# First image: layer-0 input halves seven chunks ahead, row ends ahead of the statistics, Newton steps of two images on VectorE

## What is computed

```python
x = x + _L0_conv_ref(_gn(x), w_fft_real, w_fft_imag, rot_w, rot_b, bn_gamma, bn_beta)
x = x + _L1_conv_ref(_gn(x), weight)
```

## Time and profile before

| | |
|---|---|
| median of 3 runs | 1798.08 us (1795.96 to 1798.11) |
| profiled execution, its own time | 1799.18 us |
| its span in the trace | 1797.4 us |
| mean granted PE clock (share of 2.4 GHz) | 0.977 |
| PE busy | 1655.8 us (92%) |
| DVE busy | 1388.3 us (77%) |
| ACT busy | 1172.3 us (65%) |
| POOL busy | 128.1 us (7%) |
| chain that ended last | PE 72%, DVE 14%, issue 5%, DMA 5% |
| L500 hi0, ACT | 264 of 1137 ns |
| L684 lo0, DVE | 264 of 1259 ns |
| L848 lo1, DVE | 264 of 1262 ns |
| L886 bn_stats, DVE | 454 of 687 ns |

### The profile page before, as it was taken

How to read it: one execution, slowest core, us unless ns; L and a number is a source line. 1 busy time by engine, 2 the same in 40 slices (tenths; PEclk the granted TensorE clock), 3 DMA queues, 4 the chain that set the end, 5 groups by cost and what they waited for, 6 DMA issues and landing times.

```text
span 1797.4 us, 65352 instructions
## 1 busy us (share of the span) xinstructions
PE 1655.8 (92%) x29275; PEld 1246.7 (69%) x29275; DVE 1388.3 (77%) x2175; ACT 1172.3 (65%) x1044; POOL 128.1 (7%) x361
## 2 busy tenths in 40 slices
PE   5887888487779999999999999999999999999899
PEld 5787888333356667887688668866786678666655
DVE  6989999779878787877887888787888788787500
ACT  6888888468556666666666666666666666666444
POOL 0000000120110010002000200020002001100100
PEclk9999999789899999999999999999999999999999
DMA  9999999355446665656666666566656665665245
GB/s 386 421 422 422 422 422 422 146 156 152 126 138 212 206 193 192 218 190 197 207 207 203 188 211 211 198 191 214 202 193 198 206 207 192 202 206 193 96 193 201
DMA packets 101782, 411.56 MB, mean 229 GB/s; under 512 B 16883, under 2 KB 19496, under 8 KB 85160
## 3 DMA queue, kind: packets, MB, share of 16 engines
q1 hardware_dynamic: 100744, 407.81, 64.6%
q0 software_dynamic: 800, 0.15, 0.1%
HBM read 271.82 MB, written 136.07 MB: 227 GB/s over the span
## 4 chain that ended last, share of the span: by engine, by line
PE 72%; DVE 14%; issue 5%; DMA 5%; POOL 1%; ACT 1%; SPq 1%; DVEq 0%; POOLq 0%; ACTq 0%
PE ps L406 36%; PE ps L399 34%; DVE x L635 7%; DMA x<-x_pix 5%; DVE nat L684 2%; DVE x L848 2%; DVE stats L886 1%; ACT x L475 1%; PE ps L350 0%; PE ps L351 0%; SPq L248 0%; PE ps L358 0%; POOL sm L606 0%; DVE ps L854 0%; PE ps L354 0%
## 5 line engine op out<-in xcount | busy, mean ns | idle before, releaser
L399 PE MATMUL ps<-nat,wc 64*64 64x512 f16 (+1 forms) x12480 | 1269.1, 379 | 45.7 <-DVE nat L684 16.5
L406 PE MATMUL ps<-x,wc 64*64 64x512 f16 (+2 forms) x12585 | 1256.4, 375 | 15.3 <-POOL x L615 14.8
L399 PEld LDWEIGHTS ps<-nat,wc 64*64 64x64 f16 x12480 | 721.8, 107 | 252.6 <-issue 38.2
L406 PEld LDWEIGHTS ps<-x,wc 64*64 64x64 f16 x12585 | 732.2, 107 | 193.4 <-POOL x L615 18.5
L500 ACT ACTIVATE nat<-xin,gnp 128x1024 f16<-128x1024 f32 (+1 forms) x264 | 299.9, 1137 | 318.6 <-PE ps L399 306.1
L848 DVE SCALAR_TENSOR_TENSOR x<-ps,gnp,x 128x1024 f16<-128x1024 f32 (+1 forms) x264 | 333.1, 1262 | 28.7 <-ACT x L515 21.5
L530 ACT ACTIVATE outb<-ps,bias 128x1024 f32<-128x1024 f32 (+1 forms) x264 | 289.7, 1097 | 88.5 <-PE ps L406 72.8
L684 DVE SCALAR_TENSOR_TENSOR nat<-xin,gnp,nat 128x1024 f16<-128x1024 f32 (+1 forms) x264 | 332.3, 1259 | 2.0 <-ACT nat L500 1.9
L519 ACT ACTIVATE x<-ps,gnp 128x1024 f16<-128x1024 f32 (+1 forms) x231 | 252.8, 1095 | 107.1 <-DVE stats L886 106.6
L350 PE MATMUL ps<-x 128*128 128x129 f16 x2048 | 258.0, 226 | 59.3 <-DVE x L635 59.2
L635 DVE SCALAR_TENSOR_TENSOR x<-x 128x2048 bf16<-128x2048 f32 x128 | 284.1, 2285 | 17.3 <-ACT x L475 15.6
(11 more groups left out here) (125 smaller groups left out, 273.6 us busy)
## 6 DMA issues: line engine op xcount, KB each, us to landing
x<-x_pix SPq DMA_DIRECT2D x128, 1024.0 KB, 13.5
xin<-x_tiles SPq DMA_DIRECT2D x256, 512.0 KB, 3.8
out<-outb SPq DMA_DIRECT2D x256, 512.0 KB, 4.1
xin<-x_tiles SPq DMA_DIRECT2D x8, 192.5 KB, 2.4
out<-outb SPq DMA_DIRECT2D x8, 192.5 KB, 3.7
w<-taps_scratch SPq DMA_DIRECT2D x64, 8.0 KB, 1.8
w<-taps_scratch SPq DMA_DIRECT2D x28, 16.0 KB, 2.7
taps_scratch<-x POOLq DMA_DIRECT2D x21, 3.0 KB, 3.4
```

The lines of the kernel that those rows point to most:

```text
L399: return nc.tensor.matmul(ps[64 * kind:64 * kind + 64, bank, 0:w], lhs, nat[rows, xhl, a:a + w], start=first, stop=last)
L406: ins = nc.tensor.matmul(ps[64 * kind:64 * kind + 64, bank, done:done + part], lhs, x1[rows, xhl, z:z + part], start=first and done == 0, ...
```

## The change

- `NB = 3`: image 0 has seven input slots, NFIRST0 = 7, instead of four: four in `nat`, three in slots 33 to 35 of the `x1` ring, which image 0's results don't use (`nat_at`). The start of slot 4's chunk is copied behind slot 3, and that of slot 0's chunk behind slot 6 (`nat_end`), each as two instructions, one for each half; in the later images too the copy is two instructions.
- ACT does hi0 of chunks 0 to 6 ahead of its loop, DVE lo0 of 0 to 3, `weights0(0)`, then pad and lo0 of 4 to 6, then pad(7). In the loop `ahead(g)` gives g+7 up to g = 25, nothing for g = 26 to 28, and g+4 from g = 29 on.
- The buffers of the pixel phase move, so that they keep clear of what is written early.
- POOL does `row_ends(b)` before it waits for `seeded`.
- For images 0 and 7 (`ALONE`) the Newton turns and `alpha` are done by DVE (`newton1`), right behind `spread`, with `weights1` right behind that; for the others POOL does them as before.

```diff
@@ -33,7 +33,8 @@
 PASSES = [(whl, xhl, dj) for whl, xhl in ((0, 0), (1, 0), (0, 1)) for dj in range(2)]
 NX = 4
 NO = 3
-AHEAD = 4
+NB = 3
+NFIRST0 = NX + NB
 LAG = NCH + 2
 RING = NCH + 4
 RCOLS = RING * CH
@@ -41,6 +42,7 @@
 SLOTS = 4
 TRAIL = 2
 GN_EPS, BN_EPS = 1e-5, 1e-5
+ALONE = (0, B - 1)
 YS = 16.0
 WS = 64.0
 X1S = YS * WS
@@ -106,6 +108,13 @@
     if _g >= LAG:
         JOB1[_g - LAG] = len(JOBS)
         JOBS.append((1, _g - LAG))
+
+
+def ahead(g):
+
+    if g + NFIRST0 < NCH:
+        return g + NFIRST0
+    return g + NX if g + NX >= NCH and g + NX < ALL else None
 
 
 def l1_chunk(h):
@@ -158,12 +167,14 @@
             return big[0:parts, a:a + width]
 
         apix = early(ASLOTS * ACHUNK).rearrange("p (s n) -> p s n", s=ASLOTS)
+        assert at_[0] + 256 <= NCH * CH // 2
+        TAPS_AT = at_[0]
+        tapsb = early(256, 9 * B)
+        at_[0] = RCOLS // 2
         gmask = early(B * P).rearrange("p (b q) -> p b q", b=B)
         colsum, gcol, gtmp = early(B), early(1), early(P)
         gram = early(B * C, C).rearrange("p (b c) -> p b c", b=B)
         zpad = early(400)
-        tapsb = early(256, 9 * B)
-        TAPS_AT = at_[0]
         early(at_[0] % 2)
         alo = early(AROUND * ACHUNK // 2).bitcast(BF16).rearrange("p (s k c) -> p s k c", s=AROUND, k=ABLK)
         ahi = early(AROUND * ABLK * (P + 2) // 2).bitcast(F16).rearrange("p (s k c) -> p s k c", s=AROUND, k=ABLK)
@@ -172,8 +183,8 @@
         wfs = early(256, 2 * K3)
         zt, zu = early(9 * B, 2 * K3), early(9 * B, 2 * K3)
         zc = early(384)
-        assert at_[0] <= RCOLS
-        TAPS_SLOT = min((TAPS_AT - 256) // (CH // 2), RING - 1)
+        assert at_[0] <= RCOLS // 2 + NCH * CH // 2
+        TAPS_SLOT = TAPS_AT // (CH // 2)
 
         def c(name, parts=P):
             if name in COL:
@@ -270,6 +281,19 @@
 
             return (g % RING) * CH
 
+        def nat_at(g):
+
+            spot = g % NFIRST0 if g < NCH else g % NX
+            return (nat, spot * CH) if spot < NX else (x1, (NCH + spot - NX) * CH)
+
+        def nat_end(g):
+
+            if g < NCH and g % NFIRST0 == 0:
+                return (x1, (NCH + NB) * CH)
+            if (g % NFIRST0 == NX) if g < NCH else (g % NX == 0):
+                return (nat, NX * CH)
+            return None
+
         @block.sync
         def _(sp):
             for dst, src in ((cst[:, :], consts), (first, firsts), (rw[:, :], rotw), (smallp[:, :], small),
@@ -395,8 +419,9 @@
                 bank = CB * (job % SLOTS) + q
                 lhs = (wc0 if layer == 0 else wc1)[rows, (i // NCH) % 2, whl, kind, dj, :]
                 if layer == 0:
-                    a = (i % NX) * CH + off
-                    return nc.tensor.matmul(ps[64 * kind:64 * kind + 64, bank, 0:w], lhs, nat[rows, xhl, a:a + w],
+                    planes, a = nat_at(i)
+                    a += off
+                    return nc.tensor.matmul(ps[64 * kind:64 * kind + 64, bank, 0:w], lhs, planes[rows, xhl, a:a + w],
                                             start=first, stop=last)
                 a = x1_slot((i // NCH) * NCH + n) + off
                 done = 0
@@ -495,9 +520,11 @@
                 b, n = divmod(g, NCH)
                 w = CH if n < NFULL else EDGE
                 act.wait_ge(pad_done, g + 1)
-                if g >= NX:
-                    act.wait_ge(pe_done, JOB0[g - NX] + 1)
-                nc.scalar.activation(nat[:, 0, (g % NX) * CH:(g % NX) * CH + w], xin[:, g % NX, 0:w], ACT.Identity,
+                last = g - (NFIRST0 if g < NCH else NX)
+                if last >= 0:
+                    act.wait_ge(pe_done, JOB0[last] + 1)
+                planes, a = nat_at(g)
+                nc.scalar.activation(planes[:, 0, a:a + w], xin[:, g % NX, 0:w], ACT.Identity,
                                      scale=gnp[:, 1, b:b + 1]).then_inc(hi0_ready, 1)
 
             def hi1(g):
@@ -530,14 +557,14 @@
                 nc.scalar.activation(outb[:, h % NO, 0:writes(n)], psum_of(JOB1[h], writes(n)), ACT.Identity,
                                      bias=bias[:, b % 2:b % 2 + 1], scale=1.0 / (HS * X1S)).then_inc(o_done, 1)
 
-            for g in range(NX):
+            for g in range(NFIRST0):
                 hi0(g)
             for g in range(ALL + LAG):
                 early = g < ALL and g >= NCH and by_act(*divmod(g, NCH))
                 if early:
                     hi1(g)
-                if g + NX < ALL:
-                    hi0(g + NX)
+                if ahead(g) is not None:
+                    hi0(ahead(g))
                 if g < ALL and not early:
                     hi1(g)
                 if g >= LAG:
@@ -600,13 +627,14 @@
                     upto = TROWS if n == NFULL else (n + 1) * CH // PITCH
                     column_ends(b, rows, upto)
                     rows = upto
+                row_ends(b)
                 pool.wait_ge(seeded, b + 1)
-                for turn in range(3):
-                    link(G.tensor_scalar(stat["h"], stat["y"], stat["half"], stat["y"], ALU.mult, ALU.mult))
-                    link(G.tensor_scalar(stat["y"], stat["h"], 1.5, stat["y"], ALU.add, ALU.mult))
-                G.tensor_scalar(stat["alpha"], stat["y"], X1S, gnp[:, 4, b:b + 1], ALU.mult, ALU.mult
-                                ).then_inc(alpha_ready, 1)
-                row_ends(b)
+                if b not in ALONE:
+                    for turn in range(3):
+                        link(G.tensor_scalar(stat["h"], stat["y"], stat["half"], stat["y"], ALU.mult, ALU.mult))
+                        link(G.tensor_scalar(stat["y"], stat["h"], 1.5, stat["y"], ALU.add, ALU.mult))
+                    G.tensor_scalar(stat["alpha"], stat["y"], X1S, gnp[:, 4, b:b + 1], ALU.mult, ALU.mult
+                                    ).then_inc(alpha_ready, 1)
                 link(G.tensor_scalar(stat["cc"], stat["d"], stat["M"], gnp[:, 5, b:b + 1], ALU.add, ALU.mult))
                 link(G.tensor_copy(chl[:, 0:1], stat["cc"]))
                 link(G.tensor_tensor(chl[:, 1:2], stat["cc"], chl[:, 0:1], ALU.subtract))
@@ -679,14 +707,17 @@
 
                 b, n = divmod(g, NCH)
                 w = CH if n < NFULL else EDGE
-                a = (g % NX) * CH
+                planes, a = nat_at(g)
+                end = nat_end(g)
                 ve.wait_ge(hi0_ready, g + 1)
-                ins = V.scalar_tensor_tensor(nat[:, 1, a:a + w], xin[:, g % NX, 0:w], gnp[:, 1, b:b + 1],
-                                             nat[:, 0, a:a + w], ALU.mult, ALU.subtract)
-                if g % NX == 0:
-
+                ins = V.scalar_tensor_tensor(planes[:, 1, a:a + w], xin[:, g % NX, 0:w], gnp[:, 1, b:b + 1],
+                                             planes[:, 0, a:a + w], ALU.mult, ALU.subtract)
+                if end is not None:
+
+                    copy, z = end
                     after(post(ins))
-                    ins = V.tensor_copy(nat[:, :, NX * CH:NX * CH + NXT], nat[:, :, 0:NXT])
+                    for part in range(2):
+                        ins = V.tensor_copy(copy[:, part, z:z + NXT], planes[:, part, a:a + NXT])
                 ins.then_inc(lo0_ready, 1)
 
             count = [0]
@@ -971,6 +1002,15 @@
                 V.tensor_scalar(stat["y"].bitcast(I32), stat["seed"].bitcast(I32), -1.0, float(0x5f3759df), ALU.mult, ALU.add
                                 ).then_inc(seeded, 1)
 
+            def newton1(b):
+
+                ve.wait_ge(seeded, b + 1)
+                for turn in range(3):
+                    after(post(V.tensor_scalar(stat["h"], stat["y"], stat["half"], stat["y"], ALU.mult, ALU.mult)))
+                    after(post(V.tensor_scalar(stat["y"], stat["h"], 1.5, stat["y"], ALU.add, ALU.mult)))
+                V.tensor_scalar(stat["alpha"], stat["y"], X1S, gnp[:, 4, b:b + 1], ALU.mult, ALU.mult
+                                ).then_inc(alpha_ready, 1)
+
             def weights1(b):
 
                 ve.wait_ge(alpha_ready, b + 1)
@@ -991,20 +1031,22 @@
                 lo0(g)
             for part in range(4):
                 weights0(0, part)
-            pad(NX)
+            for g in range(NX, NFIRST0):
+                pad(g)
+            for g in range(NX, NFIRST0):
+                lo0(g)
+            pad(NFIRST0)
             for g in range(ALL + LAG):
                 b, n = divmod(g, NCH)
                 if g > LAG and (g - LAG - 1) % NCH == 0:
                     biased((g - LAG - 1) // NCH)
-                if g == ALL:
-                    weights1(B - 1)
                 if g >= ALL:
                     continue
                 masked = mask(g)
                 if n == NFULL:
                     post(V.tensor_copy(stat["kp"], psum_of(JOB0[g], CH)[:, TAIL:TAIL + 1]))
-                elif g + NX + 1 < ALL:
-                    pad(g + NX + 1)
+                if ahead(g + 1) is not None:
+                    pad(ahead(g + 1))
                 after(masked)
                 sums(g)
```

(10 more changed lines are left out.)

## The result

The changed kernel takes 1789.07 us (median of 6 runs, 1786.71 to 1790.84), the one before, on the same chip, 1798.09 us (6 runs, 1795.96 to 1798.46). The ratio is 0.9951, with a 95% interval of 0.9938 to 0.9964: 9.0 us less (6.5 to 11.1 by the interval), where 6.9 were forecast. The profiled execution took 1786.71 us, the fastest of the six and 2.4 us under their median; that of before stood 1.1 us above its own. So the two traces differ by 12.5 us, and 9.0 of them stand for the kernels.

What follows compares the result with a forecast made beforehand. PE is fully busy between borders, so time falls only where it idles or runs at half clock; DVE paces the first image. 3.4 + 0 + 0 + 3.5 = 6.9 us less gives 1791.2 us; range 1786 to 1796.5.

Steps and rivals of the forecast that it cites:

- Part A: Image 0, seven chunks ahead: DVE's loop steps shorten, 3.4 us less; bounds 0 and 5.7.
- The six short waits: DVE's waits for PE between steps 1 and 25 of image 0 go: 6 x 0.3 = 1.8 us.
- The pair of copies: Slot-end copy as two half-width instructions in image 0: 0.1 us more per copy, 0.6 us in all.
- the input wait: DVE's 0.7 us stall for an input load in image 0 stays, 0.2 us longer.
- Cover of the preparation: Ahead of image 0's loop: added pads and lo0 fit in DVE's 9.3 us wait, costing nothing; 4 us without it.
- rival 3: Little gained: Newton no faster on DVE, late loads of chunks 5 to 9 eat part A; 1797 us, chance 0.10.
- Part B: Handover from image 0 to 1: PE's 7.83 us idle goes, a wait for lo1 replaces it; 0 us.
- Part C: Middle images: POOL's row ends first and Newton later change nothing; double copies lie beside PE; 0 us.
- Rival 4: Slower: POOL's later Newton holds DVE in images 1 to 6, 1.8 us each; 1802 us, chance 0.07.
- Part D: Image 7's end: Newton on DVE and row ends first let PE start 3.5 us earlier; bounds 1.4 and 4.2.
- the clock: Image 7: PE still restarts at half rate after shorter idle; 0 us gained, upper bound 2.4 more.
- The 3.37 us row: Earlier profile's PE idle of 3.37 us followed by half rate, 24 matmuls in 2.77 us; taken as nearest for image 7.

Runs made afterwards that it cites:

- a_only: Changed kernel with only seven chunks ahead in image 0; Newton, weights1 and row ends back where they were: 1794.53 us, ratio 0.9975 to the kernel before.
- slack28: Changed kernel plus two unread DVE instructions, 0.88 us, in step 28 of image 0: 1792.02 us, a single run.
- newton7: Changed kernel with image 0's Newton back on POOL and weights1(0) back in step 34; DVE does only image 7's: 1789.0 us, ratio 0.9949 to the kernel before.
- bd_only: Kernel before (four chunks ahead, single copies) with Newton on DVE in images 0 and 7 and row ends first: 1793.96 us, ratio 0.9972.
- best_nofill: Changed kernel with image 0's Newton on POOL and one slot-end copy in the middle images, no unread matmuls: 1789.44 us, ratio 0.9949 to the kernel before.
- alone_all: Changed kernel with Newton and weights1 right behind the seed on DVE in all eight images: 1814.02 us, ratio 1.0076 to the kernel before.
- rows_only: Changed kernel with Newton and alpha on POOL in all images, row ends still ahead of the seed: 1791.52 us, ratio 0.9956 to the kernel before.

## Why the prediction was right, and where it was not

Direction and range held, and the mechanism of each of the four parts was in the main the one that ran. The sum was 2.1 us short, which is within the measurement's interval of 2.3 us either way.

- **Part A, 3.4 us.** The profile shows 3.35 from step 0 to step 29 (a_only alone 3.00). The 3.35 is the best of the table's traces with seven ahead, which gave 2.4 to 3.35, so that it meets the 3.4 so closely is partly luck. By pieces: 2.43 in steps 25 to 29, where 2.7 were forecast, and PE's jobs pace them (slack28). From step 1 to step 25 81.56 became 80.56, 1.0 forecast 0.8. The six short waits went: DVE waits for PE in steps 27 and 29 and once more before 480 us. The pair of copies costs 0.06 us more than one, taken as 0.1; the input wait was 0.83, forecast 0.9. In the table's other traces with seven ahead it was 0.9 to 1.8, and steps 0 to 29 were longer by about as much more: the wait for inputs is what varies in this part.
- **Cover of the preparation.** "They cost nothing, as long as inputs 4 to 6 have landed": they had not, and 3.4 us of waits entered. What was left of the cover was 0.37 us. The term held by a margin that I had not seen, and that was luck; rival 3 had late inputs as its cause, of chunks 5 to 9.
- **Part B, 0.** Measured 0.31 gained (seed 0 to step 35), within the bounds. PE restarted behind weights1, 3.63 us after the seed (forecast 3.6), and then waited 1.70 us for lo1(33), as forecast. Newton took 1.92 us, weights1 about 1.3; against 2.05 and 1.42. newton7 shows what the sum could not: without this part the trace is 1.0 us shorter there, so the edit itself is a loss hidden by a gain, the row ends' order.
- **Part C, 0.** bd_only gives 0.04 for all six borders with POOL's order changed, and no wait on weights1 or POOL. The 0.37 us lost are the double copies (newton7 against best_nofill: 0.41), which the prediction had put at nothing because they lie beside PE. Rival 4 did not occur; alone_all shows that a longer hold, 3.7 us of DVE time, costs 4.2 us a border, where I had priced 1.8 for an alpha that is late by that much.
- **Part D, 3.5.** Measured 3.38; PE starts 3.93 us after the seed, forecast 3.77. The difference is weights1: 1.71 us, where 1.42 and 0.2 for POOL had been allowed. Its first instruction took 0.72 us beside POOL's wrap and 0.48 at the handover, where POOL was idle.
- **The step that was wrong is the clock.** I wrote "nearest is 3.37, so the slow start stays", a term of 0 with an upper bound of 2.4. Behind 3.43 us of idle PE came back at full rate in the profiled execution, 2.4 us; bd_only came back at half rate behind the same 3.43 and had 92.81 us to the end, a loss of 1.5, and best_nofill (granted clock 0.66 in its first 5 us there) 92.95. The same held for job 35 and, at the start, for the first job, which part A's own working did not price at all. In the medians it comes to about 2.3 us, with an uncertainty as large. The 3.37 us row was one draw of a stretch that has two outcomes, and a term of half its bound would have been the better estimate.

The other row that the prediction read for this, full rate behind 1.54 us, was one draw too. bd_only has the same work up to there, the same idle times and the same moments, and its job 34 came at half rate:

```profile
484.29 5.33 PE L400 MATMUL ps<-nat,wc 64*64 64x512 f16 x48 [1.54 <-DVE nat L686]
```

Before, these 48 matmuls took 2.79 us. The rule of the Trainium skill on this ("TensorE: Matmul & The Clock Gate", Part 1), that the moment of the change to full rate differs between runs, was on record beside the term. These two traces agree: 5.33 and 2.79 us for the same job behind the same 1.54 us.

## To carry over

Where PE idles ahead of a job and nothing else paces what follows, give it matmuls that nobody reads: here they took 6.2 us off beside a better order of work (1789.44 to 1783.26), perhaps 2.1 in the changed kernel, and nothing at the start, where inputs set the pace. Before serial steps move to the engine that paces what comes next, count what then waits for it: the same edit gave 2.15 us at the end, where DVE had nothing else to do, lost about 1 at the handover in the trace, and cost 4.2 at each border in the middle. When work is moved ahead of a loop, look for when its inputs land, and not only for the idle time that it fits in.

## Of the hardware, not expected

- Idle times of PE of 3.37 to 3.44 us end at either level of the clock, at the same job (35): its first 24 matmuls took 2.77 us behind 3.44 us in rows_only and 1.49 behind 3.43 in the changed kernel. The same holds for the 1.54 us at job 34 (above). Why one or the other comes was not settled.
- Small instructions of DVE (128x1) took 0.27 and 0.21 us beside POOL's row ends in image 7 (1689.88 to 1690.79), and 0.27 and 0.21 with POOL idle at 482.31 and 482.62: no stretching. The next one with large operands (L1017) was stretched beside POOL's wrap, 0.72 against 0.48 us. The Trainium skill ("GPSIMD Engine Reference", 8. Key points) has DVE and POOL contend when DVE has two SBUF inputs; the trace agrees for the large one and shows nothing of it for the small.
- The mark at which "start" begins falls at 352.6 to 354.8 us in these executions, so some 2 us of the scatter of any two profiles have nothing to do with the change.
